# Three couples a chunk get their low parts from adding DMAs instead of from VectorE and GpSimd; the spread ring holds six groups

## The reference

```python
for idx, (W, b) in enumerate(params):           # W: (39, fk, 128); fk = 39, 64, 64
    z = jnp.einsum('bhd,bkd,hks->bsd', x0, xk, W) + b[None, :, None]
    z = jax.nn.relu(z)
    if idx != n_layers - 1:
        half = z.shape[1] // 2
        xk = z[:, :half, :]
        direct.append(z[:, half:, :])
    else:
        direct.append(z)
logit = jnp.sum(jnp.concatenate(direct, axis=1), axis=-1)
```

## Time and profile before

| | |
|---|---|
| median of three runs | 562.16 us |
| time of the profiled execution | 562.33 us |
| its span, first to last instruction | 560.5 us |
| granted TensorE clock (share of full) | 0.999 |
| TensorE busy | 551.9 us (98%) |
| VectorE busy | 535.9 us (96%) |
| GpSimd busy | 499.5 us (89%) |
| ScalarE busy | 379.4 us (68%) |

### The profile page before, as it was taken

The page is one execution under the profiler, slowest core; times in us unless marked ns, Lnnn a source line. Parts: engine busy times, 40 slices in busy tenths (PEclk is TensorE's granted clock), DMA queues, the critical chain, the costliest instruction groups (busy, mean ns, idle before and its releaser), DMA issues.

```text
span 560.5 us, 6190 instructions
## 1 busy us (share of the span) xinstructions
PE 551.9 (98%) x2008; PEld 374.9 (67%) x2008; DVE 535.9 (96%) x496; ACT 379.4 (68%) x427; POOL 499.5 (89%) x228
## 2 busy tenths in 40 slices
PE   7999999999999999999999999999999999999997
PEld 2435667667677677777767677677777767677665
DVE  4679999999999999999999999999999999999985
ACT  0436577776858767676776858777676876858662
POOL 0438899899999989999899999989999899999986
PEclk9999999999999999999999999999999999999999
DMA  8997391844828266391845828276391845826200
GB/s 326 418 408 317 132 370 34 325 191 181 344 87 331 108 254 271 146 361 30 331 183 183 342 95 333 98 262 263 150 363 29 333 177 192 333 99 215 81 1 20
DMA packets 21056, 122.17 MB, mean 218 GB/s; under 512 B 2720, under 2 KB 2976, under 8 KB 10784
## 3 DMA queue, kind: packets, MB, share of 16 engines
q1 hardware_dynamic: 20736, 121.51, 56.0%
q10 hardware_dynamic: 288, 0.26, 0.2%
HBM read 121.24 MB, written 0.52 MB: 217 GB/s over the span
## 4 chain that ended last, share of the span: by engine, by line
PE 82%; DVE 10%; issue 3%; ACT 2%; DMA 1%; POOL 1%; SPq 0%; DVEq 0%; POOLq 0%; ACTq 0%
PE z L611 82%; DVE raw L426 4%; DVE exact L426 3%; DVE d_raw L426 2%; DMA fields<-x_fields 1%; DVE lo L440 1%; POOL lo L515 1%; ACT hi L656 1%; ACT maps L675 0%; ACT final L696 0%; ACT L675 0%; DVE sums L453 0%; DVE sums L447 0%; SPq L358 0%; SPq L337 0%
## 5 line engine op out<-in xcount | busy, mean ns | idle before, releaser
L515 POOL TENSOR_TENSOR lo<-raw,hi 128x1024 fp32r<-128x1024 f32 x198 | 469.1, 2410 | 12.1 <-ACT hi L656 11.6
L656 ACT ACTIVATE hi<-raw 128x1024 fp32r<-128x1024 f32 (+1 forms) x213 | 219.1, 1029 | 125.1 <-DVE raw L426 112.0
L611 PE MATMUL z<-hi,w_hi 128*128 128x512 f32 (+1 forms) x559 | 220.8, 399 | 0.9 <-ACT hi L656 0.4
L426 DVE TENSOR_TENSOR raw<-spread,maps 128x1024 f32<-128x1024 f32 x184 | 219.0, 1210 | 2.1 <-ACT maps L675 2.1
L611 PE MATMUL z<-hi,w_lo 128*128 128x512 f32 x513 | 202.5, 395 | 0.0
L611 PE MATMUL z<-lo,w_hi 128*128 128x512 f32 x544 | 196.7, 451 | 0.2 <-POOL lo L515 0.2
L611 PE MATMUL z<-exact,w_exact 128*128 128x512 f32 (+1 forms) x386 | 180.4, 594 | 2.8 <-DVE exact L426 2.0
L611 PEld LDWEIGHTS z<-lo,w_hi 128*128 128x128 f32 x544 | 101.2, 188 | 56.2 <-issue 31.5
L611 PEld LDWEIGHTS z<-hi,w_hi 128*128 128x128 f32 (+1 forms) x559 | 104.8, 188 | 31.4 <-ACT final L696 3.7
L611 PEld LDWEIGHTS z<-exact,w_exact 128*128 128x128 f32 (+1 forms) x386 | 72.1, 189 | 68.0 <-issue 53.7
L611 PEld LDWEIGHTS z<-hi,w_lo 128*128 128x128 f32 x513 | 96.2, 188 | 22.9 <-issue 0.5
(11 more groups left out here) (21 smaller groups left out, 69.6 us busy)
## 6 DMA issues: line engine op xcount, KB each, us to landing
spread<-x_spread SPq DMA_DIRECT2D x80, 1024.0 KB, 8.1
fields<-x_fields SPq DMA_DIRECT2D x31, 768.0 KB, 6.8
fields<-x_fields SPq DMA_DIRECT2D x15, 512.0 KB, 5.6
w_exact<-w SPq DMA_DIRECT2D x10, 256.0 KB, 14.7
spread<-x_fields SPq DMA_DIRECT2D x1, 768.0 KB, 10.1
raw<-w SPq DMA_DIRECT2D x1, 640.0 KB, 6.7
spread<-x_fields SPq DMA_DIRECT2D x1, 512.0 KB, 10.7
out<-sums SPq DMA_DIRECT2D x2, 240.0 KB, 4.2
```

The lines of the kernel that those rows point to most:

```text
L426: nc.vector.tensor_tensor(products, by_field, by[0:rows, :].unsqueeze(1).to_broadcast([rows, tiles, COLS]), ALU.mult).then_inc(ready, 1)
L515: nc.gpsimd.tensor_tensor(low_part(layer, c, k), raw[low_rows(layer, k), PLACE[S][layer, c, k] % RAW_RING, 0:tiles_in(layer, k), :], hi[lo ...
L611: mm = nc.tensor.matmul(z_of(layer, c)[:, :], w[0:rows, :], part[0:rows, :], start=(step == FIRST_STEP[layer, c] and p == 0), stop=(step = ...
L656: nc.scalar.activation(hi[0:rows, count % HI_RING, 0:tiles, :], products, ACT.Copy).then_inc(hi_ready, 1)
```

## The change

- A fourth kind **A**: the product goes to `raw` and ScalarE rounds it to `hi` as for S. ScalarE then writes the negated product, rounded to fp32r, into a new ring `added` (two couples). GpSimd issues a DMA that adds the raw product to it in SBUF, so that raw - hi stands there. TensorE's lo pass waits for that DMA. The pass comes `A_LAG` = 4 couples after the hi pass.
- In chunks 1 to 15, layer 0 is DSES instead of SDES, layer 1 DSASAESSES instead of ESDSESSDSS, layer 2 SSEDASSEDS instead of SSDSSESDES. A chunk goes from 14 S, 5 D, 5 E to 12 S, 3 A, 4 D, 5 E. Chunk 0 keeps its numbers of each kind but not their places.
- Rings: `exact` 4 to 3, `hi` 5 to 6, `spread` 7 to 6. Lags: layer 0's low parts follow at once (2 to 0), layer 1's after 2 couples (from 1), VectorE's own after 2 (from 3). `KEPT` goes from 7 to 8, the places of maps, sums and copies move.
- GpSimd's order is `POOL_ORDER`, by the couple after which each low part is due, since adds and subtractions are now in one queue.

```diff
-KINDS = ("SDES", "ESDSESSDSS", "SSDSSESDES")
-KINDS_FIRST = ("EEEE", "ESEEEEEEEE", "EESEEESEES")
+KINDS = ("DSES", "DSASAESSES", "SSEDASSEDS")
+KINDS_FIRST = ("EEEE", "EEEEEEESEE", "EEESESEEES")
-LO_LAGS = (2, 1, 1)
-D_LAG = 3
-EXACT_RING = 4
+LO_LAGS = (0, 2, 1)
+ADD_LAG = 1
+A_LAG = 4
+D_LAG = 2
+EXACT_RING = 3
 RAW_RING = 6
-HI_RING = 5
+HI_RING = 6
 LO_RING = 4
-SPREAD_RING = 7
+SPREAD_RING = 6
-SUM_LAST_AT = 6
-SUM_DIRECT_AT = 6
-COPY_AT = 2
+SUM_LAST_AT = 8
+SUM_DIRECT_AT = 8
+COPY_AT = 7
 FINISH_AT = 2
-MAPS1_AT = 5
-MAPS2_AT = 3
-KEPT = 7
+MAPS1_AT = 6
+MAPS2_AT = 2
+KEPT = 8
...
-                pending.append((at + LO_LAGS[layer], layer, c, k))
+                pending.append((at + (A_LAG if kind == A else LO_LAGS[layer]), layer, c, k))
...
+POOL_ORDER = sorted((couple for couple in LOW if couple in PLACE["SA"]),
+                    key=lambda couple: (AT[couple] + ADD_LAG if couple in PLACE[A] else
+                                        max(AT[c] for c in LOW[:USED[couple] + 1] if c in PLACE[S])
+                                        + LO_LAGS[couple[0]]))
...
+        added = sb("added", [128, 2, 2, COLS], fp32r)
...
+        def wait_added(engine, couple):
+            place = PLACE[A][couple]
+            engine.wait_ge(a_lo_ready[place % 2], 16 * (place // 2 + 1))
...
+            def add_low(layer, c, k):
+                place = PLACE[A][layer, c, k]
+                pool.wait_ge(negated_ready, place + 1)
+                if place >= 2:
+                    wait_added(pool, COUPLE[A][place - 2])
+                nc.gpsimd.dma_start(low_part(layer, c, k),
+                                    raw[:, PLACE["SA"][layer, c, k] % RAW_RING, :, :],
+                                    accum_op=ALU.add).then_inc(a_lo_ready[place % 2], 16)
...
+                        elif kind == A:
+                            wait_added(pe, (layer, c, k))
...
                     nc.scalar.activation(hi[0:rows, count % HI_RING, 0:tiles, :], products,
                                          ACT.Copy).then_inc(hi_ready, 1)
+                    if kind == A:
+                        if PLACE[A][layer, c, k] >= 2:
+                            act.wait_ge(lo_used, USED[COUPLE[A][PLACE[A][layer, c, k] - 2]] + 1)
+                        nc.scalar.activation(low_part(layer, c, k), products, ACT.Copy,
+                                             scale=-1.0).then_inc(negated_ready, 1)
```

More of the change, by code:

```diff
@@ L22 @@
 LAYER_TILES = (TILES0, TILES, TILES)
-E, S, D = "E", "S", "D"
-KINDS = ("SDES", "ESDSESSDSS", "SSDSSESDES")
-KINDS_FIRST = ("EEEE", "ESEEEEEEEE", "EESEEESEES")
+E, S, D, A = "E", "S", "D", "A"
+KINDS = ("DSES", "DSASAESSES", "SSEDASSEDS")
+KINDS_FIRST = ("EEEE", "EEEEEEESEE", "EEESESEEES")
 EARLY = 2
@@ L50, in tiles_of @@
     return [t for t in range(LAYER_TILES[layer]) if any(kinds(layer, c)[t // 2] in wanted for c in (0, 1, 2))]
-SPLIT_TILES = [tiles_of(n, S + D) for n in range(3)]
+SPLIT_TILES = [tiles_of(n, S + D + A) for n in range(3)]
 assert SPLIT_TILES[0][:-1] == list(range(len(SPLIT_TILES[0]) - 1)) and SPLIT_TILES[0][-1] == TILES0 - 1
 assert KINDS[0][-1] != E and KINDS_FIRST[0] == E * COUPLES[0]
-assert all(KINDS[n][-1] != E for n in (1, 2))
-LO_LAGS = (2, 1, 1)
-D_LAG = 3
-EXACT_RING = 4
+assert all(KINDS[n][-1] not in E + A for n in (1, 2)) and A not in KINDS[0]
+LO_LAGS = (0, 2, 1)
[3 more added lines that the diff above has]
+EXACT_RING = 3
 RAW_RING = 6
-HI_RING = 5
+HI_RING = 6
 LO_RING = 4
 QUADS = TILES // 4
-SPREAD_RING = 7
+SPREAD_RING = 6
 W0_CUTS = (0, 2, TILES0)
@@ L153 @@
 RUNS = [None, runs_of(1), runs_of(2)]
-PLACE = {E: {}, S: {}, D: {}, "SD": {}}
+PLACE = {E: {}, S: {}, D: {}, A: {}, "SA": {}, "SDA": {}}
 for _layer, _c, _couples in SEGMENTS:
@@ L166 @@
 USED = {couple: n for n, couple in enumerate(LOW)}
-S_LOW = {couple: n for n, couple in enumerate(c for c in LOW if c in PLACE[S])}
-assert len(USED) == len(PLACE["SD"])
+LOW_OWN = [couple for couple in LOW if couple not in PLACE[A]]
+LOW_PLACE = {couple: n for n, couple in enumerate(LOW_OWN)}
+AT = {}
+for _layer, _c, _couples in SEGMENTS:
+    for _k in _couples:
+        AT[_layer, _c, _k] = len(AT)
+POOL_ORDER = sorted((couple for couple in LOW if couple in PLACE["SA"]),
+                    key=lambda couple: (AT[couple] + ADD_LAG if couple in PLACE[A] else
+                                        max(AT[c] for c in LOW[:USED[couple] + 1] if c in PLACE[S])
+                                        + LO_LAGS[couple[0]]))
+S_LOW = {couple: n for n, couple in enumerate(c for c in POOL_ORDER if c in PLACE[S])}
+assert len(USED) == len(PLACE["SDA"])
 def pair_places():
@@ L272, in cin_kernel @@
         hi_ready = sem("hi_ready")
+        negated_ready = sem("negated_ready")
+        a_lo_ready = [sem("a_lo_ready0"), sem("a_lo_ready1")]
         lo_used = sem("lo_used")
@@ L283, in wait_multiplied @@
             kind = kinds(layer, c)[k]
-            engine.wait_ge({E: exact_ready, S: raw_ready, D: d_raw_ready}[kind], PLACE[kind][layer, c, k] + 1)
+            if kind == E:
+                engine.wait_ge(exact_ready, PLACE[E][layer, c, k] + 1)
+            elif kind == D:
+                engine.wait_ge(d_raw_ready, PLACE[D][layer, c, k] + 1)
+            else:
+                engine.wait_ge(raw_ready, PLACE["SA"][layer, c, k] + 1)
+        def wait_added(engine, couple):
+            place = PLACE[A][couple]
+            engine.wait_ge(a_lo_ready[place % 2], 16 * (place // 2 + 1))
         def wait_contracted(engine, layer, c):
@@ L296, in wait_high_free @@
             if count >= HI_RING:
-                engine.wait_ge(lo_used, USED[COUPLE["SD"][count - HI_RING]] + 1)
+                engine.wait_ge(lo_used, USED[COUPLE["SDA"][count - HI_RING]] + 1)
         def wait_low_free(engine, count):
             if count >= LO_RING:
-                engine.wait_ge(lo_used, count - LO_RING + 1)
+                engine.wait_ge(lo_used, USED[LOW_OWN[count - LO_RING]] + 1)
         def tiles_in(layer, k):
@@ L315, in low_part @@
             if rest(layer, k):
-                return hi[low_rows(layer, k), PLACE["SD"][layer, c, k] % HI_RING, 0:1, :]
-            return lo[:, USED[layer, c, k] % LO_RING, :, :]
+                return hi[low_rows(layer, k), PLACE["SDA"][layer, c, k] % HI_RING, 0:1, :]
+            if kinds(layer, c)[k] == A:
+                return added[:, PLACE[A][layer, c, k] % 2, :, :]
+            return lo[:, LOW_PLACE[layer, c, k] % LO_RING, :, :]
         def z_of(layer, c):
@@ L417, in multiply @@
                         products, ready = exact[0:rows, count % EXACT_RING, 0:tiles, :], exact_ready
-                    elif kind == S:
+                    elif kind in S + A:
+                        count = PLACE["SA"][layer, c, k]
                         if count >= RAW_RING:
-                            dve.wait_ge(s_lo_ready, S_LOW[COUPLE[S][count - RAW_RING]] + 1)
+                            before = COUPLE["SA"][count - RAW_RING]
+                            if before in PLACE[S]:
+                                dve.wait_ge(s_lo_ready, S_LOW[before] + 1)
+                            else:
+                                wait_added(dve, before)
                         products, ready = raw[0:rows, count % RAW_RING, 0:tiles, :], raw_ready
@@ L435, in split_lo @@
             def split_lo(layer, c, k):
-                count = USED[layer, c, k]
-                place = PLACE["SD"][layer, c, k]
+                count = LOW_PLACE[layer, c, k]
+                place = PLACE["SDA"][layer, c, k]
                 dve.wait_ge(hi_ready, place + 1)
@@ L515, in split_lo @@
                 nc.gpsimd.tensor_tensor(low_part(layer, c, k),
-                                        raw[low_rows(layer, k), PLACE[S][layer, c, k] % RAW_RING,
+                                        raw[low_rows(layer, k), PLACE["SA"][layer, c, k] % RAW_RING,
                                             0:tiles_in(layer, k), :],
@@ L540, in weights0_split_lo @@
                                         ALU.subtract).then_inc(weights_lo[0], 1)
-            for layer, c, k in LOW:
-                if kinds(layer, c)[k] != S:
-                    continue
+            def add_low(layer, c, k):
[6 more added lines that the diff above has]
+                                    accum_op=ALU.add).then_inc(a_lo_ready[place % 2], 16)
+            for layer, c, k in POOL_ORDER:
                 if (layer, c) == (1, 0):
@@ L554, in _ @@
                     weights_split_lo(2, TILES)
-                split_lo(layer, c, k)
+                if kinds(layer, c)[k] == S:
+                    split_lo(layer, c, k)
+                else:
+                    add_low(layer, c, k)
         @block.tensor
@@ L571, in contract @@
                     else:
-                        count = PLACE["SD"][layer, c, k]
+                        count = PLACE["SDA"][layer, c, k]
                         if what == "hi":
@@ L588, in contract @@
```

(11 more changed lines are left out.)

## The result

The kernel after takes 614.46 us (median of 4 runs, 613.31 to 614.79) against 562.16. The ratio is 1.0925, with a 95% interval of 1.0911 to 1.0939. The profiled execution took 614.38, its span is 612.3. I had said 561.0, with 580 at most.

What follows compares the result with a forecast made beforehand. TensorE was taken as the bound, VectorE nearly so. Mid-run -0.6, head -1.6 and tail +0.9 summed to -1.3 us, giving 561.0 us; overall range 559.5 to 580.

Steps and rivals of the forecast that it cites:

- That TensorE is the bound and relief of VectorE brings nothing: Whole run: TensorE's count is 33.55 of a 33.58 us period; relieving VectorE only brings back TensorE's stalls, 6.6 us in all.
- X: Issue time of an adding DMA on GpSimd, between 0.33 and 2.4 us, taken as 1.3.
- Rival 2: GpSimd becomes the bound if X is over 2.05 us: about 576 us; chance 0.07.
- T: Landing time of a 512 KB adding DMA, between 4.2 and 8.1 us, taken as 5.6 from loads that size.
- X + T: Time an add may take: 7.2 us for 1.4, 8.4 for 1.2, 9.5 for 2.4; 6.9 forecast, all in time.
- rival 1: Adds too late for TensorE, 1.4 tightest, each us over 7.2 lost once a chunk: 568.5 to 611 us; chance 0.22.
- Brings 6.1 MB plus an add in about 16 us: Load burst from 2.1's product on; third spread group lands some 13 us behind 2.1, needed at 14.6.
- rival 3: Spread loads arrive late, one more us of delay costing 15 us: 576 us; chance 0.06.
- The tail: Chunk 15: 1.7 us lost waiting for maps, 0.8 gained in the last segment, net loss 0.9 us.
- The head: Chunk 0: stalls at layer 1's split couple, the small low pass and the wait on final go, gaining 1.6 us.
- Mid-run: TensorE's short waits on final go, 0.04 us a chunk over 14 chunks, gaining 0.6 us.
- my estimate from it, at half rate: Landing of an add inside the load burst, from the skill page's formula with both operands read: 6.8 us.

Runs made afterwards that it cites:

- e8: Kernel before, VectorE making its low parts over half their columns from chunk 3 on: 561.77 us, ratio 0.9990.
- e6: Kernel after, each add moving only 16 columns of one tile (128 rows of 64 B): 563.75 us, ratio 1.0029.
- e4: Kernel after, SyncE issuing the next chunk's fields behind all groups of spread: 589.85 us, ratio 1.0477.
- e13: As e4, with layer 2's couple 4 split by GpSimd in place of an add: 567.59 us, ratio 1.0087.
- e2: Kernel after, adds running in full but TensorE's low pass of those couples reading hi without waiting for them: 613.39 us (one run).
- e11: As e6, but the add moves its 16 columns in 32 partitions only: 563.74 us (one run).
- e7: Kernel before, with layer 1's one split couple in chunk 0 moved from place 1 to place 7: 561.92 us, ratio 0.9995.
- e1: Kernel after, each add moving 16 of 512 columns of both tiles: 586.47 us, ratio 1.0414.
- e14: As e13, with 1.2 split by GpSimd too, so only 1.4's add stays: 568.07 us, ratio 1.0103.
- e9: Kernel after, spread rows in HBM with gaps, so loads move 2 KB pieces in place of 8 KB: 629.84 us, ratio 1.1212.

## Why the prediction was wrong, step by step

*That TensorE is the bound and relief of VectorE brings nothing*: right. e8 shows it from the side of VectorE, e6's 33.53 us from that of TensorE.

*X, the issue on GpSimd*: taken as 1.3, it is 0.87. Rival 2 is out; GpSimd's share fell to 77%.

*T, the landing*: this step failed. I took 5.6 us from the loads of 512 KB, for all three adds alike. That value holds for 1.4 (5.8), for 1.2 it is 9.0 and for 2.4 10.2. I had noted that 2.4's add stands inside the burst and then gave it the median of loads, 13 of 15 of which had one or two others in flight when they were issued. 2.4's add is mostly issued with five or six in flight. X + T of 11.1 is over 9.5 for 2.4, 9.9 over 8.4 for 1.2, and 6.7 under 7.2 for 1.4, so 1.4, which I called the tightest, is the one in time. That is rival 1's mechanism at another couple. By my own price the excess of 2.4 in e4 is (0.87 + 10.5 - 9.5) x 15 = 28 us, and e4 is 27 over before. e13 shows that couple: without 2.4's add 22 of the 27 us go.

*"Brings 6.1 MB plus an add in about 16 us"*: failed too. 6.1 MB at 2.65 us a MB are 16.2 us by themselves, so the add stood in my count at next to nothing. It occupies the 16 engines for 2.65 us, as 1 MB does, and two adds fall into the burst. The third to fifth groups had 1 us of room or little more in my count and 2 us of VectorE's lead behind it. 5.3 us more in front of them is over both, by about 2 to 3 us. VectorE waits up to 2.7. That is rival 3, to which I gave 0.06; e2 shows that it alone gives 613. e4 shows that the queue's order was about half of the loss: `fields` stood in front of groups that are needed first. The seventh slot of the ring was given up too, and no run has the adds with seven groups, so how much that would have saved is open.

*Two rivals together*: the losses don't add up. Late loads alone give 51 us (e2), late adds alone 27 (e4), both 52. An argument for it, not tested by itself: while TensorE's producers wait for a load, the adds land. I had priced each rival alone, which was right, but as alternatives.

*The tail*: TensorE waits 1.81 us for the last maps, 2.0 were forecast. From `final` of chunk 13 to the last one e11 takes 558.5 - 511.2 = 47.3 us, before 557.3 - 511.4 = 45.9: a loss of 1.4, 0.9 forecast. *The head*: 1.6 forecast as a gain; e7 gives 0.4 for the largest part, within its noise, and e6 is 0.5 us behind before at the third `final` (142.56 against 142.05). In e6 VectorE waits 1.2 and 0.2 us for loads there; with the fields last (e4, e13) `final` of chunk 0 starts at 74.0, 0.9 earlier than before. *Mid-run*: 0.6 forecast as a gain, and from the third `final` to that of chunk 13 e6 makes up 0.5 us; this term was right. So with harmless adds the change costs 1.4 us (563.75 against 562.34 measured beside it) where I had forecast a gain of 1.3.

The Trainium skill's page "DMA: Bandwidth & Descriptors" (§ Queues, rings and completion order) says that an engine takes turns between its queues a packet at a time, a packet being typically 9 to 17 descriptors. The taking of turns agrees with e6, e11 and e1. The size of a turn does not, if a descriptor is a piece of the trace: a turn is one piece here. 14 more pieces an engine cost 4.3 us, 0.31 each, and one 8 KB piece of a load occupies its engine for about 0.0082 x 2.65 x 16 = 0.35. Its 2.0 us plus size (§ Anatomy of one DMA) agrees with 1.9 to 2.5 for the small adds behind the burst; for 512 KB with both operands counted it gives an estimate of 4.4, and e14's trace shows 4.3. For adds in the burst my estimate from it, at half rate, was 6.8, and the traces show 10.2 for 2.4.

The add with 3 pieces takes 4 us more in the burst than its 1.9. About 3 of them lie in front of its first piece: it goes 4.3 us after the issue (281.09 to 285.38) with the engines on loads alone, and in quiet 1.4 us after it (e6, 294.52 to 295.9). The rest are its three turns. That the engines first finish loads which they had already fetched would fit, but no run tells that apart.

## What to carry to other kernels

Price a DMA by where in the load pattern it is issued: a window of the DMA share around the issue, not the median landing, and then ask which load it pushes back. An add within SBUF occupies the engines as a load of twice its size. When an engine sits at its floor in the trace, work taken off its neighbour is worth what the floor leaves, here 0.6 us, and each new wait is a risk with no prize.

## What the runs showed of the hardware that I had not expected

- In a saturated stretch a DMA's landing is a wait in front of its first piece, 4.3 to 4.6 us in four kernels here (1.4 in quiet), and then one piece of a load for each of its pieces on an engine. For small pieces the number counts and not the bytes: 16 KB in 256 pieces took 10.2 us, 8 KB in 128 pieces 7.6, 2 KB in 32 pieces 5.9. With pieces of 4 KB their own 0.33 us come on top: 512 KB in 128 pieces took 10.2.
- An adding DMA takes 2.65 us of all 16 engines for 512 KB, a plain copy within SBUF 1.42, a load from HBM 1.39 (0.524 MB at 2.65 us). GpSimd's issue takes 0.87 for the add and 0.57 for the copy.
- A VectorE instruction of 64x128 between two SBUF tiles took 0.29 us in e9 (at 33.3 us) and 6.32 in e14 beside GpSimd's back-to-back subtractions, where its record runs to the end of GpSimd's work.
